# Mean times deviation by a column product, a seventh decay buffer and a new timetable, in a state-space layer kernel

## What is computed

```python
h = layernorm(x) * (1 + ca) + sa
xs, z = split(h @ w_in.T + b_in);  z = silu(z)
dt = softplus(xs @ w_dt.T + b_dt);  Bm, Cm = xs @ w_B.T + b_B, xs @ w_C.T + b_C
# 16 states per feature, 512 features, one step per row:
hst = exp(A * dt) * hst + dt * Bm * xs;   y = sum(hst * Cm, states)
y = (y + D * xs) * z @ w_out.T + b_out
x = x + ga * layernorm(y + h) * gamma + beta
h = layernorm(x) * (1 + cb) + sb
x = x + gb * (small feed-forward of h)
```

## Time and profile before

| what | value |
|---|---|
| median of 3 runs | 4452.8 us (4450.74 to 4457.69) |
| the profiled execution | 4458.12 us |
| its span, first to last instruction | 4456.4 us |
| mean granted TensorE clock | 0.969 of full |
| busy: PE, ACT, DVE, POOL | 92%, 86%, 84%, 82% |

### The profile page before, as it was taken

The page is one execution under the profiler, slowest core; times in us unless marked ns, Lnnn a source line. Parts: engine busy times, 40 slices in busy tenths (PEclk is TensorE's granted clock), DMA queues, the critical chain, the costliest instruction groups (busy, mean ns, idle before and its releaser), DMA issues. The chain is left out here.

```text
span 4456.4 us, 68965 instructions
## 1 busy us (share of the span) xinstructions
PE 4097.4 (92%) x21664; PEld 2562.2 (57%) x21664; DVE 3759.8 (84%) x5133; ACT 3825.2 (86%) x6371; POOL 3664.6 (82%) x2218
## 2 busy tenths in 40 slices
PE   7999999999999999999999999999999999999987
PEld 3655565655565555655555656555655555555554
DVE  3788888888888888888888888888888888888884
ACT  3888898888898888988888988888988889888884
POOL 2898888888888888888888888888888888888883
PEclk8899999999999999999999999999999999999998
DMA  4566665666665666666676656666656666656764
GB/s 148 115 140 152 142 147 123 143 145 150 147 147 121 144 149 146 146 132 129 142 157 141 145 124 138 145 149 147 139 124 148 150 147 145 135 129 141 158 135 85
DMA packets 260961, 622.84 MB, mean 140 GB/s; under 512 B 31068, under 2 KB 33116, under 8 KB 260600
## 3 DMA queue, kind: packets, MB, share of 16 engines
q0 software_dynamic: 117248, 369.14, 45.5%
q1 hardware_dynamic: 143352, 249.29, 17.3%
HBM read 281.70 MB, written 34.64 MB: 71 GB/s over the span
## 5 line engine op out<-in xcount | busy, mean ns | idle before, releaser
L411 POOL TENSOR_TENSOR work<-work,c_bc 128x1024 f32<-128x1024 f32 x1024 | 2618.5, 2591 | 455.8 <-DVE work L1218 268.0
L1218 DVE TENSOR_TENSOR_SCAN work<-work,state,b_ps 128x512 f32<-128x512 f32 x1792 | 2235.4, 1271 | 223.7 <-PE b_ps L526 212.5
L925 ACT ACTIVATE work<-u_td,b_td 128x512 f32<-128x512 f32 x2048 | 1453.6, 710 | 99.4 <-PE b_ps L526 90.5
L915 ACT ACTIVATE work<-dt_t,neg_a 128x512 f32<-128x512 f32 x2048 | 1451.7, 709 | 43.7 <-DVE work L1218 43.7
L526 PE MATMUL b_ps<-ident,work 128*128 128x128 f32 x8192 | 1231.2, 280 | 246.6 <-DVE work L1218 188.7
L526 PEld LDWEIGHTS b_ps<-ident,work 128*128 128x128 f32 x8192 | 979.9, 144 | 812.8 <-DVE work L1218 410.8
L601 PEld LDWEIGHTS y_ps<-ident,work 128*128 128x128 f32 x4096 | 475.6, 143 | 123.8 <-issue 122.8
L422 POOL DMA_DIRECT2D work<-work x512 | 492.5, 1013 | 60.6 <-POOL work L411 41.6
L601 PE MATMUL y_ps<-ident,work 128*128 128x128 f32 x4096 | 536.3, 276 | 0.7 <-DMA work<-work 0.7
L704 PE MATMUL dense<-h_t,w_in_t 128*128 128x512 f32 x1024 | 523.5, 638 | 1.0 <-ACT h_t L929 1.0
L675 PE MATMUL dense<-w_out_t,proj 128*128 128x512 f32 x1024 | 515.8, 606 | 0.0
(11 more groups left out here) (112 smaller groups left out, 4366.2 us busy)
## 6 DMA issues: line engine op xcount, KB each, us to landing
work<-work POOLq DMA_DIRECT2D x512, 512.0 KB, 5.6
c_bc<-c_d SPq DMA_DIRECT2D x512, 256.0 KB, 3.4
xn<-in_x SPq DMA_DIRECT2D x128, 256.0 KB, 7.0
work<-xs_t POOLq DMA_DIRECT2D x64, 512.0 KB, 7.7
x<-in_x SPq DMA_DIRECT2D x128, 256.0 KB, 5.2
x<-par_d POOLq DMA_DIRECT2D x64, 512.0 KB, 7.3
x<-par_d POOLq DMA_DIRECT2D x32, 1024.0 KB, 10.8
out_dram<-x SPq DMA_DIRECT2D x128, 256.0 KB, 4.1
```

Of the source, the lines that this page charges most:

```text
L411: gp.tensor_tensor(made_here, both(hs, HS_RING, s * U + i), c_bc[:, (s * N + n) % C_RING:(s * N + n) % C_RING + 1, :].to_broadcast([P, 2, ...
L915: A(decay[:, (s * U + i) % DEC_RING, :], dt_t[:, s % 2, j, :], ACT.Exp, scale=neg_a[:, j, n:n + 1]).then_inc(S["dec_done"], 1)
L925: A(v[:, n % V_RING, tb, :], u_td[:, tb, :], ACT.Copy, scale=b_td[:, s % 2, tb, n:n + 1]).then_inc(S["v_done"], 1)
L1218: V.tensor_tensor_scan(hs[:, (s * U + i) % HS_RING, :], decay[:, (s * U + i) % DEC_RING, :], b_ps[:, i % 2, :], state[:, i:i + 1] if s % N ...
```

## The change

The instruction of line 1231 becomes a reduce with a product over the columns 6, 8 and 10 of `norm`: the mean, r, and a new column that holds -1, set once at the start. For this r and the logarithm change places (r to column 8, the logarithm and later -m * r to 9) in all three norms, and `norm` gets 11 columns. The decay ring has seven buffers instead of six, so ACT stands one decay further ahead. Nearly every entry of the timetable moves, most by one to three slots.

```diff
-    V_RING, DEC_RING, HS_RING, PR_RING, C_RING = 2, 6, 6, 12, 3
+    V_RING, DEC_RING, HS_RING, PR_RING, C_RING = 2, 7, 6, 12, 3
...
-        store=(9, 12, 12, 15),
-        load=(13, 13, 16, 18),
+        store=(1, 9, 18, 18),
+        load=(12, 12, 19, 19),
...
-        xsh=(18, 23),
-        x1=(24, 24, 25, 28),
+        xsh=(17, 22),
+        x1=(22, 22, 27, 27),
...
-        dt_add=(41, 47, 50, 51),
-        u_mul=(47, 50, 51, 51),
+        dt_add=(43, 49, 49, 50),
+        u_mul=(47, 49, 50, 50),
...
-        skip=(3, 13, 13, 13),
-        rstdx=17,
-        xn=(17, 17, 17, 18),
-        t2=(17, 18, 21, 24),
+        skip=(0, 3, 5, 5),
+        rstdx=15,
+        xn=(15, 15, 15, 15),
+        t2=(14, 18, 25, 29),
...
-        y_copy=(6, 6, 6, 6),
+        y_copy=(4, 4, 4, 4),
...
-        out=(14, 15, 17, 19),
-        pre=(14, 17, 20, 23),
-        dt=(41, 46, 50, 50),
-        ut=(56, 57, 58, 59),
-        z=(27, 53, 57, 62),
+        out=(12, 13, 15, 17),
+        pre=(12, 15, 18, 24),
+        dt=(41, 45, 49, 49),
+        ut=(55, 56, 57, 58),
+        z=(27, 52, 56, 62),
...
-        stx=(9, 14, 15, 15),
-        nmrx=16,
-        st2=(28, 29, 31, 31),
+        stx=(5, 5, 12, 13),
+        nmrx=14,
+        st2=(25, 30, 30, 31),
         nmr2=31,
-        y=(16, 16, 17, 17, 31, 31, 33, 34, 41, 42, 42, 44, 54, 54, 54, 54, 55, 56, 56, 56, 57, 62, 62, 62, 62, 62, 62, 62, 62, 66, 69, 69),
+        y=(18, 20, 22, 23, 31, 31, 32, 32, 44, 45, 45, 45, 51, 53, 54, 54, 54, 55, 56, 56, 61, 61, 63, 63, 63, 63, 63, 63, 63, 64, 65, 66),
...
-        norm = sb("norm", [P, 3, TB, 10])
+        norm = sb("norm", [P, 3, TB, 11])
...
-                A(norm[:, 2, :, 8:9], norm[:, 2, :, 7:8], ACT.Ln, bias=eps[:, :]).then_inc(S["ln2_done"], 1)
+                A(norm[:, 2, :, 9:10], norm[:, 2, :, 7:8], ACT.Ln, bias=eps[:, :]).then_inc(S["ln2_done"], 1)
...
-                A(norm[:, 2, :, 9:10], norm[:, 2, :, 8:9], ACT.Exp, scale=-0.5).then_inc(S["rstd2_done"], 1)
+                A(norm[:, 2, :, 8:9], norm[:, 2, :, 9:10], ACT.Exp, scale=-0.5).then_inc(S["rstd2_done"], 1)
...
             V.memset(eps[:, :], EPS)
+            V.memset(norm[:, :, :, 10:11], -1.0).then_inc(S["sign_set"], 1)
...
                 dve.wait_ge(S[rstd], at(rstd, k, 1))
-                V.scalar_tensor_tensor(norm[:, n, :, 8:9], norm[:, n, :, 6:7], -1.0, norm[:, n, :, 9:10], ALU.mult,
-                                       ALU.mult).then_inc(S[nmr], 1)
+                dve.wait_ge(S["sign_set"], 1)
+                V.tensor_reduce(norm[:, n, :, 9:10], norm[:, n, :, 6:11:2], mybir.AxisListType.X, ALU.mult
+                                ).then_inc(S[nmr], 1)
```

More of the change, by code:

```diff
@@ L35, in build_program @@
     PE_AT = {}
[L36 to L45, removed]
+    for entry in """g.0@0 g.1@3 g.2@3 g.3@3 g.4@3 g.5@4 g.6@6 yz.0@6 g.7@6 res.0@7 yz.1@7 pre.0.0@8 yz.2@8 pre.0.1@9
+        yz.3@9 pre.0.2@10 out.0@11 pre.0.3@11 res.1@11 pre.1.0@11 out.1@13 pre.1.1@14 pre.1.2@14 out.2@14
+        pre.1.3@14 res.2@16 pre.2.0@16 out.3@16 pre.2.1@16 pre.2.2@17 pre.2.3@17 res.3@17 xt.0@19 pre.3.0@19
+        pre.3.1@21 pre.3.2@23 pre.3.3@23 z.0.0@25 xt.1@25 z.0.1@25 z.0.2@26 xt.2@26 z.0.3@26 xs.0.0@28
+        xt.3@28 xs.0.1@28 xs.0.2@29 xs.0.3@29 xs.1.0@29 xs.1.1@29 xs.1.2@29 xs.1.3@30 xs.2.0@32 xs.2.1@32
+        xs.2.2@32 xs.2.3@32 xs.3.0@33 xs.3.1@33 x2.0@35 xs.3.2@35 xs.3.3@36 dt.0.0@37 dt.0.1@37 x2.1@38
+        dt.0.2@39 dt.0.3@40 dt.1.0@41 dt.1.1@42 x2.2@42 dt.1.2@42 dt.1.3@42 dt.2.0@43 dt.2.1@44 x2.3@46
+        dt.2.2@46 dt.2.3@48 dt.3.0@48 dt.3.1@48 dt.3.2@48 dt.3.3@48 cb.0@49 cb.1@49 cb.2@49 cb.3@50 z.1.0@50
+        z.1.1@50 bt.0@50 z.1.2@51 z.1.3@51 z.2.0@52 ut.0@56 z.2.1@56 z.2.2@56 ut.1@56 z.2.3@56 s.0@57 ut.2@57
+        s.1@57 s.2@57 ut.3@57 s.3@57 z.3.0@58 z.3.1@58 z.3.2@60 z.3.3@60""".split():
         part, first = entry.split("@")
@@ L48, in build_program @@
     AT = dict(
-        store=(9, 12, 12, 15),
-        load=(13, 13, 16, 18),
-        c_store=51,
-        xsh=(18, 23),
-        x1=(24, 24, 25, 28),
-        bout=57,
-        dt_add=(41, 47, 50, 51),
-        u_mul=(47, 50, 51, 51),
-        gate=(29, 54, 57, 10),
-        relu=(61, 62, 2, 2, 2, 5, 7, 7),
-        gm=8,
-        skip=(3, 13, 13, 13),
-        rstdx=17,
-        xn=(17, 17, 17, 18),
-        t2=(17, 18, 21, 24),
+        store=(1, 9, 18, 18),
+        load=(12, 12, 19, 19),
@@ L64, in build_program @@
+        c_store=47,
+        xsh=(17, 22),
+        x1=(22, 22, 27, 27),
+        bout=53,
+        dt_add=(43, 49, 49, 50),
+        u_mul=(47, 49, 50, 50),
+        gate=(28, 60, 62, 7),
+        relu=(61, 62, 1, 3, 3, 3, 4, 4),
+        gm=6,
+        skip=(0, 3, 5, 5),
+        rstdx=15,
+        xn=(15, 15, 15, 15),
+        t2=(14, 18, 25, 29),
         rstd2=32,
         xn2=(32, 32, 32, 32),
[L66 to L75, removed]
-        y_copy=(6, 6, 6, 6),
-        yz=(9, 10, 11, 12),
-        out=(14, 15, 17, 19),
-        pre=(14, 17, 20, 23),
-        dt=(41, 46, 50, 50),
-        ut=(56, 57, 58, 59),
-        z=(27, 53, 57, 62),
+        h2=(36, 39, 42, 46),
+        h=(20, 26, 27, 29),
+        xs=(30, 31, 34, 37),
+        cb=50,
+        bt=50,
+        edt=(43, 48, 49, 51),
@@ L83, in build_program @@
+        ldt=(43, 48, 49, 51),
+        ez=(29, 54, 58, 4),
+        lz=(29, 54, 58, 6),
+        sig=(29, 54, 58, 6),
+        y_copy=(4, 4, 4, 4),
+        yz=(6, 8, 9, 10),
+        out=(12, 13, 15, 17),
[3 more added lines that the diff above has]
+        z=(27, 52, 56, 62),
         s=59,
-        stx=(9, 14, 15, 15),
-        nmrx=16,
-        st2=(28, 29, 31, 31),
+        stx=(5, 5, 12, 13),
+        nmrx=14,
+        st2=(25, 30, 30, 31),
         nmr2=31,
-        y=(16, 16, 17, 17, 31, 31, 33, 34, 41, 42, 42, 44, 54, 54, 54, 54, 55, 56, 56, 56, 57, 62, 62, 62, 62, 62, 62, 62, 62, 66, 69, 69),
@@ L89, in build_program @@
-        sum=(5, 8, 10, 14, 14, 16, 17, 19, 23, 23, 30, 34, 34, 37, 42, 45, 46, 48),
+        y=(18, 20, 22, 23, 31, 31, 32, 32, 44, 45, 45, 45, 51, 53, 54, 54, 54, 55, 56, 56, 61, 61, 63, 63, 63, 63, 63, 63, 63, 64, 65, 66),
+        sum=(5, 8, 9, 11, 14, 16, 18, 21, 25, 25, 30, 34, 34, 38, 41, 43, 45, 48),
     )
@@ L200, in build_program @@
         w2dg_done b_out_loaded bout_done moved_ps moved c_exp c_one c_rcp silu_c rows_ps rows_taken mods_ps mods_done sign_done gate_done par_made
-        par_stored bout_row bout_made bout_added gs_loaded wg_loaded wout_done""".split()
+        par_stored bout_row bout_made bout_added gs_loaded wg_loaded wout_done sign_set""".split()
         PER = {
@@ L977, in normalize @@
                 act.wait_ge(S["mvx_done"], at("mvx_done", f, TB))
-                A(norm[:, 0, :, 8:9], norm[:, 0, :, 7:8], ACT.Ln, bias=eps[:, :]).then_inc(S["lnx_done"], 1)
+                A(norm[:, 0, :, 9:10], norm[:, 0, :, 7:8], ACT.Ln, bias=eps[:, :]).then_inc(S["lnx_done"], 1)
                 act.wait_ge(S["lnx_done"], at("lnx_done", f, 1))
-                A(norm[:, 0, :, 9:10], norm[:, 0, :, 8:9], ACT.Exp, scale=-0.5).then_inc(S["rstdx_done"], 1)
+                A(norm[:, 0, :, 8:9], norm[:, 0, :, 9:10], ACT.Exp, scale=-0.5).then_inc(S["rstdx_done"], 1)
                 for tb in range(TB):
@@ L984, in normalize @@
                         act.wait_ge(S["nmrx_done"], at("nmrx_done", f, 1))
-                    A(xn[:, tb, :], xn[:, tb, :], ACT.Identity, scale=norm[:, 0, tb, 9:10],
-                      bias=norm[:, 0, tb, 8:9]).then_inc(S["xn_done"], 1)
+                    A(xn[:, tb, :], xn[:, tb, :], ACT.Identity, scale=norm[:, 0, tb, 8:9],
+                      bias=norm[:, 0, tb, 9:10]).then_inc(S["xn_done"], 1)
             def attend(b):
@@ L991, in attend @@
                     act.wait_ge(S["mvp_done"], at("mvp_done", b, tb + 1))
-                    A(norm[:, 1, tb, 8:9], norm[:, 1, tb, 7:8], ACT.Ln, bias=eps[:, :]).then_inc(S["lnp_done"], 1)
+                    A(norm[:, 1, tb, 9:10], norm[:, 1, tb, 7:8], ACT.Ln, bias=eps[:, :]).then_inc(S["lnp_done"], 1)
                     act.wait_ge(S["lnp_done"], at("lnp_done", b, tb + 1))
-                    A(norm[:, 1, tb, 9:10], norm[:, 1, tb, 8:9], ACT.Exp, scale=-0.5
+                    A(norm[:, 1, tb, 8:9], norm[:, 1, tb, 9:10], ACT.Exp, scale=-0.5
                       ).then_inc(S["rstdp_done"], 1)
@@ L997, in attend @@
                     act.wait_ge(S["t1_done"], at("t1_done", b, tb + 1))
-                    A(tmp[:, tb, :], tmp[:, tb, :], ACT.Copy, scale=norm[:, 1, tb, 9:10]
+                    A(tmp[:, tb, :], tmp[:, tb, :], ACT.Copy, scale=norm[:, 1, tb, 8:9]
                       ).then_inc(S["t2_done"], 1)
@@ L1011, in normalize_second @@
                         act.wait_ge(S["xt_ps"], at("xt_ps", f, KD))
-                    A(xn[:, tb, :], x1[:, tb, :], ACT.Identity, scale=norm[:, 2, tb, 9:10],
-                      bias=norm[:, 2, tb, 8:9]).then_inc(S["xn2_done"], 1)
```

(2 more changed lines are left out.)

## The result

The changed kernel takes 4426.12 us (median of 4 runs, 4425.9 to 4429.25) against 4454.47 us of the kernel before: ratio 0.9938, 95% interval 0.9921 to 0.9955. That is 28 us where 161 were forecast, and it lies above the range.

A forecast was written before the change was run, and what follows sets the result against it. No engine is full; waits bound the step, chiefly DVE's line 1231 blocked by POOL. For the profiled execution 4458.1 - 119 - 45 + 31 - 30 + 3 = 4298 us; stated as a median of 4292 us, range 4212 to 4375.

The forecast's parts named there:

- The reading of the block: DVE line 1231, second norm: its 4.19 us are a block by POOL, not work; a reduce would not be held.
- the sum had 119: DVE line 1231: replacing the instruction by a reduce removes 129.1 us and adds 10.2, a gain of 119 us.
- the clock's 45 us: PE after the block: the slow clock costs 1.6 us in some 28 steps, a gain of 45 us, bounds 0 to 75.
- the charge of 31 for giving back: POOL falls further behind DVE without the block, so u is late for PE: 1 us a step, 31 us cost.
- Until POOL has run out of ready work: DVE line 1231: the block lasts over several POOL instructions in a row, 4.19 us, until POOL has none ready.
- The 80 us that I worked out by the rule alone: DVE line 1231: if the block ended with POOL's current instruction, at most 2.6 us, removing it gives some 80 us.
- Store, load and shift earlier: SP's stores and loads, POOL's shift: DVE's 41.3 us wait for x1 shrinks, 30 us won, bounds 0 and 41.
- The other slots I count 0, with 1 us a step either way: Remaining moved timetable entries: no effect, with 32 us either way.
- SP's list: SP's first store at slot 1 delays the C row behind it; a tie with DVE's slot 12, 3 us cost in all.
- The ring: Decay ring of seven buffers: ACT's wait for a scan stays the same and DVE hardly waits for decays, 0 us.
- Given back: Rival, chance 0.20: without the block, PE's and POOL's backlog bounds the step and returns about half the gains: 4378 us.
- the sign that I had named for it: Would show gains given back: DVE's waits for PE at lines 1302 and 1218 grow by over 60 us together.

The follow-up runs named there:

- e1: The kernel before with only the reduce and its columns, old timetable and ring of six: 4319.83 us, 0.9675.
- e2: The changed kernel with the old instruction put back, new timetable and ring of seven kept: 4487.7 us, 1.0049.
- e19: The changed kernel with SP's second pair of stores and loads at their slots of before and the old instruction put back: 4301.36 us, 0.9645.
- e13: The changed kernel with only SP's second pair of stores and loads back at their slots of before: 4266.73 us, 0.9572.
- e8: The changed kernel with SP's first pair of stores and loads at their slots of before, second pair still late: 4374.82 us, 0.9816.
- e14: The changed kernel with POOL's second shift at slot 25 instead of 22, behind the first two adds; stores and loads stay late: 4293.22 us, 0.9627.
- e16: The changed kernel with SP's second pair back, and PE's adds (but the last three) and POOL's sums at their slots of before: 4457.95 us, 0.9996.
- e7: The changed kernel with SP's stores and loads at their slots of before, except the first store, kept at slot 1: 4288.06 us, 0.9614.
- e5: The kernel before with the reduce and the decay ring of seven, old timetable: 4311.19 us, 0.9671.
- e18: The changed kernel with SP's second pair at its slots of before and the decay ring of six: 4271.9 us, 0.9579.

## Why the prediction was wrong, point by point

**The reading of the block was right in its main point:** it is no work, and the reduce isn't held. Of the 139 us that e1 measured, 118.5 are DVE's lost busy time at this line (129.1 to 10.6); the sum had 119. The rest, some 20 us, is what the clock's 45 us and the charge of 31 for giving back came to together, where the sum had 14. From the block's end to the first norm's instruction it took 96.4 us in the mean before (93.8 to 97.5) and takes 95.7 in e1 (94.4 to 97.4): 0.7 us a step for the two together. The slow clock behind the reduce is gone (1.00 in e1 from 2099 to 2103 us, behind the reduce of 2097.43), and ACT's wait at line 1012 fell from 126.2 to 7.6 us. No run has the two terms apart, so that their sum came out near is in part luck.

"Until POOL has run out of ready work" isn't shown. In the kernel before, in e2 and in e19 this instruction was held 92 times, and each time it ended within 0.05 us of the end of a product after which POOL paused for 0.3 us or more, 2.5 to 2.6 in the kernel before. By the rule of the Trainium skill that I set against the rows (SBUF — State Buffer, § Who interferes with whom: the one that issues first holds the ports for its instruction) the block should end with the instruction that it met. The blocks that began inside a product agree (0.89 us in e19). Those that began in a gate do not: the gate of the earlier trace rows ended at 2031.21, and the block at 2034.45. The 80 us that I worked out by the rule alone were too little for the old timetable, where 139 were measured.

**The step that failed** is "Store, load and shift earlier. ... I take 30 of the 41.3 as won", with its bounds "0 and 41". I priced where x1 went (24 to 22) and the first pair of loads, and not the second pair, which went from 16 and 18 to 19 behind stores moved to 18, nor that the second shift, due at 22, stands in POOL's list ahead of the adds due at 22, nor that the statistics moved from 28 to 25, in front of them. These moves were in the diff. The late second pair carries 159 us (e13; 84 us where the first pair is back too, e8), and the shift ahead of the adds 133 (e14); these are two ways to undo one loss and don't add up. So this term had the wrong sign. The sum had a gain of 27 us for the timetable (30 less SP's 3), and it lost 106 (4426 - 4320). POOL's wait at line 446 rose from 144.1 to 158.3 us instead of falling well under 144. The page of before had the numbers for the sign (KB each, median us to landing):

```profile
x<-in_x SPq DMA_DIRECT2D x128, 256.0 KB, 5.2
x<-par_d POOLq DMA_DIRECT2D x64, 512.0 KB, 7.3
...
out_dram<-x SPq DMA_DIRECT2D x128, 256.0 KB, 4.1
```

Here they stand one after the other. A store at slot 18 and the load behind it take 9.3 us by these medians, and from slot 18 to the shift's slot 22 there are four slots of 2.1 us (135.0 / 64), 8.4 us; so by this estimate the shift has to wait. The step shown took longer: from the first store's issue at 1985.45 to the shift's at 2000.88 it is 15.4 us, with two stores and two loads in turn.

**"The other slots I count 0, with 1 us a step either way"** was too narrow, both ways. Beside the late second pair a single slot of `xsh` is worth 133 us (e14), the slots of adds and sums are worth 191 (e16), and the other new slots gain 3.3 us a step in the stretch after the second norm, about 100 us that the sum had at 0. In a timetable written out by hand a slot has no price of its own, and the 80 us of spread that I gave to all of them was less than one had.

**SP's list:** the tie fell against me, POOL did wait for the C row (108.4 us in all). The charge of 3 us holds where the second pair is in time (e7, e13). In the changed kernel itself up to 51 us may hang on it (e8), which isn't shown. **The ring** was right (e5, e18). **Given back** was the right direction, with a chance of 0.20, by a mechanism that isn't the one: by the sign that I had named for it, DVE's waits for PE at lines 1302 and 1218 should have grown by over 60 us, and they fell from 330.7 to 305.2 (lines 1304 and 1219 now); and e1 gives nothing back. The price it had, 4378, was still 48 us too low.

## What to carry to other kernels

When a stall is removed and the order is rewritten at once, price them apart: the stall from its rows, and of the order each list in turn, with what is queued ahead of the first instruction that the next engine needs. A moved load counts by its last consumer, with all DMAs in between, and a wait matters by where it stands: 110 us of POOL's waits for the C row were free (e7, e13), and 50 us less of DVE's waits went with 133 us of time (e14). If the parts can be run apart, the better half may beat the whole, as it did here by 2.4%.

## What was not expected of the hardware

The same DVE instruction on 128x4 elements, with two operands in SBUF, takes 0.16 us where no tensor operation of POOL runs beside it, 0.89 us when it comes at the end of a POOL product (e19), and 4.19 us when it comes in a gate that a DMA issue and a product follow (before). In e2 it even waited when it came during POOL's DMA issue, before the product had begun; DVE, then POOL:

```profile
2185.91 3.10 DVE L1233 SCALAR_TENSOR_TENSOR norm<-norm 128x4 f32<-128x4 f32 x1 [1.42 <-ACT norm L1006]
```

```profile
2185.71 0.87 POOL L422 DMA_DIRECT2D work<-work  x1 [0.30 <-POOL work L411]
2186.32 2.65 POOL L411 TENSOR_TENSOR work<-work,c_bc 128x1024 f32<-128x1024 f32 x1
```

Ten of e2's 29 blocks are of this kind, 2.70 to 3.12 us long. Yet in two other steps of the same run the instruction took 0.17 us within 0.1 us of such an issue's start, and in the first norm of the kernel before it took 0.16 us beside a DMA issue of line 429. What decides between the two isn't shown. The length of such a block is set by the order on the other engine, so its removal is worth 139 us in one timetable, 62 in another (e2 against the changed kernel) and 35 in a third. DVE's busy time saved at this line is 118.5, 63.0 and 26.5 us in the same three.
